# Layer two of a graph network: three picked tiles in every superblock, 64-slot bins in column halves, rows returned as PSUM sums

## The chip, the cores and the metric

The kernel is one program on one core of a Trainium2 chip. Its engines are TensorE (PE in the rows, its weight loads PEld), VectorE (DVE), ScalarE (ACT), GpSimd (POOL) and SyncE (SP), which run side by side and wait for each other by semaphores. The metric is the time of one execution on the device in microseconds, the median of several runs.

## What is computed

Two layers on a graph of 6250 nodes and 200000 edges, the edges sorted by target. Layer one is a normalised sum over neighbours. Layer two, which the change is about, forms a message for every edge and sums the messages by target:

```python
x = x + _L0_gnn_ref(h, edge_index, L0_gnn_W, L0_gnn_b)        # layer one
h = jnp.maximum(_layernorm(x, axis=-1), 0.0)
...
source_x = jnp.take(node_x, sources, axis=0)                  # layer two
target_x = jnp.take(node_x, targets, axis=0)
message_in = jnp.concatenate((source_x, target_x, edge_x), axis=1)
message_x = relu(message_in @ msg_W1 + msg_b1) @ msg_W2 + msg_b2
agg = jax.ops.segment_sum(message_x, targets, num_segments=num_nodes)
update_in = jnp.concatenate((agg, node_x), axis=1)
return relu(update_in @ upd_W1 + upd_b1) @ upd_W2 + upd_b2
```

The source part of the first product is made once for every node: a table a of 6250 rows of 64 numbers. A message before its ReLU is then the source's row of a, plus the target's row of a second table b, plus the edge's own features times a 64x64 weight.

## The kernel before

**Tiling.** Edges are taken in tiles of 128 (one edge a partition) and in superblocks of T = 8 tiles, NSB = 196 superblocks in all. Four superblocks (U = 4, slots k = 0 to 3) make one trip of the loop that every engine runs over layer two, 49 trips. Each engine has its instructions in an order written out by hand (`step`), with parts of later superblocks ahead of those of the current one.

**Two ways to a source row.** Most tiles are gathered: POOL issues one indirect DMA for each tile of 128 rows (L684), from indices that SP loads. Of every 32 tiles POOL gathers 22 (slots 0 and 1 whole, six tiles of slot 3). The other ten (all of slot 2, two of slot 3; `KPE`, `PT`, `GTS`) are picked on PE, in two groups g of five tiles a trip. A group's 640 edges are put into 7 bins of source nodes (896 nodes each) with 128 slots a bin, by ranks that are worked out ahead of layer one. One group then takes these stages:
- DVE marks each edge's slot and bin (L1093 to L1096), PE packs the sources into slots (`pack_slots`, L1727: five products of 7 columns), DVE copies them (L1101);
- PE spreads them over the partitions (`spread_slot_src`, L1738: seven transposing products of 128 columns), ACT copies (L1405);
- DVE builds the one-hot matrices `pick` (L1109: seven of 896 columns), PE multiplies them with the table a held in bf16 in three parts (`pick_rows`, L1760: 49 products, 128 slots by 192 columns), ACT copies (L1414);
- DVE builds `from_slot` (L1118: seven of 640 columns), PE brings the rows from slots back to edges (`return_rows`, L1774: 5 tiles by 7 bins = 35 products of 192 columns), DVE adds the three parts into `rows` (`build_rows`, L1127).

**A superblock's own work.** SP loads its edge features, indices and window of b. DVE writes its target one-hots (L905). PE transposes both together (`transpose_edges`, L1692: 8 fp32 products of 128 columns) two steps ahead, ACT copies them (L1392). `edge_and_target_terms` (L1702) makes 16 fp32 products of 64 columns into bank 2 or 3; each has 64 weight columns and fills one half of the partitions, left and right half in turn, and the trace shows two instructions for each fp32 product with a 64-wide weight, 32 in all. DVE adds the source rows (`add_rows`, L1137), ACT applies ReLU (L1397), PE sums the messages by target (`sum_messages`, L1712: 8 such products, 16 instructions), DVE adds the window's sums into `acc` (L1144).

**Order.** In PE's step k: `spread_slot_src` if k is even, then `transpose_edges`, then `pack_slots` and half of `pick_rows` if k is odd, `edge_and_target_terms`, then `return_rows` (k even) or the rest of `pick_rows` (k odd), then `sum_messages`. DVE is strictly in order: `add_rows` stands ahead of picks, copies and one-hots of later superblocks.

**Ahead of layer one.** POOL works out bins and running counts (L626 to L648), PE the ranks (L1518, L1519), ACT copies them, POOL forms codes and the crowding flag (L651 to L678). If a bin held more edges than slots, layer two would be repeated in rounds (`ROUNDS`).

## Time and profile before

| | |
|---|---|
| median of 3 runs | 2338.83 us (2332.95 to 2340.99) |
| the profiled execution | 2333.39 us, of it 2331.6 us in the span of its profile |
| set-up up to the first gather of layer one | 0 to 199 us |
| layer one | 199 to 800 us |
| between the layers | 800 to 863 us |
| layer two, 196 superblocks | 863 to 2293 us |
| update and output | 2293 to 2332 us |
| busy shares of the span | PE 88%, PEld 77%, DVE 72%, POOL 70%, ACT 49% |

The busy time of a stretch of PE reaches from its first product's start to its last one's modelled end, and a single product lasts far longer than the distance to the next one, so distances are worked out from starts. For POOL a gather counts as busy while it is prepared; what passes between two gathers is put down as idle time with the releaser "issue". A letter "ld" behind PE means weight loads. A wait names the engine and line that came last.

### The profile page before, as it was taken

Reading aid. Unit: us, or ns where it says so; the run is one execution under the profiler, and the core shown is the slowest. Engines: PE = TensorE matmul, PEld = TensorE weight load, DVE = VectorE, ACT = ScalarE, POOL = GpSimd, SP = SyncE. Lnnn points to the kernel's source line nnn. Section 1 sums busy time; section 2 is a strip of 40 time slices with the busy share of each in tenths; the row PEclk is TensorE's granted clock in tenths of the full one; section 3 lists DMA queues with packets and bytes.
Section 4 is the critical chain, followed back from the end, with each engine's and each line's share of the span. In section 5 each row is a group of like instructions: output and inputs, shape, how many; then the busy total and the mean of one; then the engine's idle time right before and its main releaser. Section 6 shows DMA issues by size and latency. Waiting matters only on the chain.

```text
span 2331.6 us, 79009 instructions
## 1 busy us (share of the span) xinstructions
PE 2043.8 (88%) x26825; PEld 1784.7 (77%) x26826; DVE 1687.9 (72%) x4590; ACT 1147.5 (49%) x2411; POOL 1628.0 (70%) x1577
## 2 busy tenths in 40 slices
PE   2156999999999949999999999999999999999997
PEld 1144788887888748888888888888888888888884
DVE  8866788887888686776667666666666677666662
ACT  0003888888888644444444444444444444444432
POOL 4465777777777127777777777777777777777771
PEclk6566999999999969999999999999999999999998
DMA  3001111111111133333333333333333333333332
GB/s 75 1 1 42 27 27 28 28 28 28 25 27 28 9 76 68 78 80 74 75 75 75 75 75 75 75 75 75 75 75 75 77 78 76 74 74 74 76 73 39
DMA packets 346919, 133.38 MB, mean 57 GB/s; under 512 B 305501, under 2 KB 322755, under 8 KB 346787
## 3 DMA queue, kind: packets, MB, share of 16 engines
q1 hardware_dynamic: 298980, 82.66, 15.9%
q0 software_dynamic: 47808, 49.05, 11.7%
q8 instruction: 72, 1.18, 0.2%
q14 instruction: 59, 0.48, 0.1%
HBM read 124.04 MB, written 7.52 MB: 56 GB/s over the span
## 4 chain that ended last, share of the span: by engine, by line
PE 54%; DVE 15%; issue 13%; POOL 10%; DMA 4%; DVEq 3%; ACT 1%; SPq 1%; POOLq 0%; PEld 0%; PEldq 0%; ACTq 0%
PE psum L1570 12%; PE psum L1760 12%; POOL rows L684 9%; PE psum L1602 9%; DVE H L1109 4%; PE psum L1774 4%; PE psum L1702 4%; PE psum L1712 3%; PE psum L1591 2%; DMA rows<-a_rows,idx 2%; PE psum L1692 2%; DVEq L1148 2%; DMA idx<-src_by_tile 2%; DVE rows L1127 1%; PE psum L1581 1%
## 5 line engine op out<-in xcount | busy, mean ns | idle before, releaser
L684 POOL DMA_INDIRECT rows<-a_rows,idx x1078 | 1088.9, 1010 | 374.8 <-issue 360.3
L1339 ACT ACTIVATE hT<-psum 128x392 bf16<-128x392 f32 x1152 | 510.6, 502 | 101.3 <-PE psum L1602 93.2
L684 POOL DMA_INDIRECT rows<-g_rows,idx x416 | 425.9, 1024 | 152.5 <-issue 125.6
L1760 PE MATMUL psum<-edge_index,H 128*128 128x192 bf16 x4802 | 429.8, 246 | 61.0 <-DVE Y L1101 59.4
L1570 PE MATMUL psum<-work,hT 128*128 128x192 bf16 x3528 | 455.9, 247 | 0.3 <-ACT hT L1339 0.3
L1760 PEld LDWEIGHTS psum<-edge_index,H 128*128 128x128 bf16 x4802 | 389.8, 98 | 70.7 <-issue 65.7
L1392 ACT ACTIVATE eoT<-psum 128x512 f32<-128x512 f32 x392 | 213.8, 603 | 351.6 <-PE psum L1692 348.0
L1570 PEld LDWEIGHTS psum<-work,hT 128*128 128x128 bf16 x3528 | 324.3, 99 | 70.9 <-issue 1.4
L1602 PE MATMUL psum<-Z,one_lo 128*128 128x392 f16 x1152 | 365.4, 339 | 14.6 <-DVE Z L946 14.5
L1414 ACT ACTIVATE Y<-psum 128x384 bf16<-128x384 f32 (+1 forms) x392 | 176.5, 450 | 308.5 <-PE psum L1760 297.3
L1774 PE MATMUL psum<-Y,Z 128*128 128x192 bf16 x3430 | 307.7, 246 | 0.9 <-ACT Y L1405 0.9
L946 DVE TENSOR_SCALAR Z<-digit,edge_index 128x392 f16<-128x392 f16 x1152 | 296.9, 328 | 0.0
L1774 PEld LDWEIGHTS psum<-Y,Z 128*128 128x128 bf16 x3430 | 285.4, 98 | 7.7 <-ACT Y L1405 1.1
L1109 DVE TENSOR_SCALAR H<-Y,node_cmp 128x896 bf16<-128x896 f16 x686 | 261.2, 451 | 6.9 <-ACT Y L1405 6.8
L1137 DVE TENSOR_TENSOR msg<-psum,rows 128x512 f32<-128x512 f32 x196 | 134.4, 686 | 149.7 <-DMA rows<-a_rows,idx 118.3
L1702 PE MATMUL psum<-wb,eoT 128*64 128x64 f32 x6272 | 226.6, 225 | 0.0
L1118 DVE TENSOR_SCALAR Z<-Z,slot_cmp 128x640 bf16<-128x640 f16 x686 | 225.3, 397 | 0.0
L1702 PEld LDWEIGHTS psum<-wb,eoT 128*64 128x64 f32 x6272 | 199.5, 138 | 31.6 <-issue 31.6
L905 DVE TENSOR_TENSOR work<-iota_bw,rel 128x512 f32<-128x512 f32 x196 | 135.7, 693 | 118.5 <-issue 118.5
L1692 PE MATMUL psum<-ident,work 128*128 128x128 f32 x1568 | 211.7, 278 | 0.0
L1602 PEld LDWEIGHTS psum<-Z,one_lo 128*128 128x128 bf16 x1152 | 160.3, 145 | 36.2 <-DVE Z L946 25.6
L1397 ACT ACTIVATE msg<-msg 128x512 f32<-128x512 f32 x196 | 123.2, 629 | 110.3 <-DVE msg L1137 94.0
(272 smaller groups left out, 1961.5 us busy)
## 6 DMA issues: line engine op xcount, KB each, us to landing
work<-in_edge_attr_dram SPq DMA_DIRECT2D x392, 128.0 KB
rows<-a_rows,idx POOLq DMA_INDIRECT x1078
Z<-slot_code SPq DMA_DIRECT2D x98, 160.0 KB
rows<-g_rows,idx POOLq DMA_INDIRECT x416
idx<-src_by_tile SPq DMA_DIRECT2D x200, 4.0 KB
wb<-b_rows SPq DMA_DIRECT2D x196, 16.0 KB, 2.3
g_rows<-Y SPq DMA_DIRECT2D x1, 1600.0 KB, 8.9
a_rows<-Y SPq DMA_DIRECT2D x6, 256.0 KB, 2.6
```

The lines of the kernel that those rows point to most:

```text
L684: pool.indirect_dma_start(out=rows[:, k, t, :], out_offset=None, in_=table, in_offset=bass.IndirectOffsetOnAxis(ap=idx[:, k, t:t + 1], axis=0)
L946: V.tensor_scalar(keys[:, g * T + t, :], key_digit[:, :], key_of[:, bass.ds(tile + t, 1)], None, ALU.is_equal).then_inc(key_ready, 1)
L1109: ins = V.tensor_scalar(pick[:, b, :], slot_src[:, :], node_cmp[:, b:b + 1], None, ALU.is_equal)
L1118: ins = V.tensor_scalar(from_slot[:, b, 0:cols], code_row[:, g, 0:cols], slot_cmp[:, b:b + 1], None, ALU.is_equal)
L1339: nc.scalar.activation(counts[:, j % 2, :, t * SLOTS:(t + 1) * SLOTS], psum[:, t % 4, 0:KEYS].rearrange("p (h m) -> p h m", m=SLOTS), ACT.Copy
L1392: nc.scalar.activation(eoT[:, k % 2, h * 4:h * 4 + 4, :], psum[:, h, :].rearrange("p (t e) -> p t e", e=P), ACT.Copy).then_inc(eoT_ready, 1)
L1570: ins = TT.matmul(psum[:, 4 + (j + 1) % 2, 0:NPART * D], counts[:, (j + 1) % 2, h, :], gtab[:, h, :, :].rearrange("p k d -> p (k d)"), sta ...
L1602: TT.matmul(psum[:, t % 4, 0:KEYS], one_lo[:, t // T, :, t % T], keys[:, t, :], start=True, stop=True).then_inc(counted, 1)
L1692: ins = TT.transpose(psum[:, h, (t % 4) * P:(t % 4 + 1) * P], eo[:, k, t, :], ident[:, :])
L1702: ins = TT.matmul(psum[half:half + D, 2 + k % 2, t * D:(t + 1) * D], eoT[:, k % 2, t, half:half + D], wb[:, k, :], start=True, stop=True)
L1760: ins = TT.matmul(psum[:, PICK_BANK[u], (b % 2) * NPART * D:(b % 2 + 1) * NPART * D], pick[:, h, b * P:(b + 1) * P], atab[:, b * BLK + h, ...
L1774: ins = TT.matmul(psum[:, bank, (t - t0) * NPART * D:(t - t0 + 1) * NPART * D], from_slot[:, b, t * P:(t + 1) * P], picked_rows[:, b, :], ...
```

## The change

Every superblock is now alike. POOL gathers its first five tiles, PE picks the last three (`PG` = 5, `PT` = 3), so a trip of four superblocks has 20 gathered and 12 picked tiles. A superblock's 384 picked edges go into 10 bins of 640 nodes with 64 slots each, two bins to a chunk of 128 slots (`CHUNKS` = 5).

- `pick_rows`: a bin's product has 64 weight columns and goes to one half of the partitions; left and right bin alternate: 5 chunks x 5 blocks x 2 halves = 50 products of 192 columns a superblock.
- `picked_tiles` takes the place of `return_rows` and `build_rows`: for each picked tile PE first writes the edge and target terms into the message bank (two fp32 products of 64 columns in halves), then adds 5 chunks x 3 parts = 15 products of 64 columns with the whole array's weights onto the same 64 columns. No DVE reduction is left; DVE adds gathered rows for five tiles only, and ACT's ReLU reads three tiles straight from PSUM.
- The stages run for every superblock (`for_stages` with offsets of up to four steps), with two buffers each. `pack_slots` now waits for the copy of the first picked bank of superblock j+2 (it shares bank 7), which stands behind `relu` of j+1 on ACT.
- In a step of PE the transposes come first, then the spread.
- Bins are found by integer shifts and one-hots on DVE, right behind the sources' transposition; the ranks are reduced by DVE out of PSUM, and POOL starts its chain after that. A product of one-hot and source for every picked edge and chunk (`chunk_src`) is made by POOL between the layers.
- SP loads indices of five tiles, one code DMA of three tiles a superblock.

The core of the diff:

```diff
-    KPE = 2
-    POOL_SLOTS = [k for k in range(U) if k != KPE]
-    GTS = (5, 5)
-    PT = sum(GTS)
-    GOFF = (0, GTS[0])
-    GT = max(GTS)
-    GE = GT * P
-    PE0 = KPE * T
-    PIECES = [([(7, 4, 1)] if n == 5 else []) + [(5, 0, 2), (6, 2, 2)] for n in GTS]
-    NPIECE = sum(len(p) for p in PIECES)
-    GATHERS = [T - max(0, min(T, PE0 + PT - k * T)) if k >= KPE else T for k in range(U)]
-    BINS = 7
-    BLK = HS // BINS
+    PT = 3
+    PG = T - PT
+    CAP = D
...
+    BINS = 10
+    BLK = 5
     BIN_NODES = BLK * P
-    SLOTS_G = BINS * P
-    NPT = NIT * PT
-    ROUNDS = GE // P
-    CENTRE = 2 * SLOTS_G
-    LAST = 4
-    LAST_BASE = 4096 - LAST * SLOTS_G + CENTRE
+    CHUNKS = BINS * CAP // P
...
+    NPT = NSB * PT
+    GE = PT * P
+    ROUNDS = GE // CAP
...
+    SPREAD_BANK = (5, 6)
+    PICK_BANK = (7, 6, 5)
+    PACK_BANK = 7
+    NPICK = len(PICK_BANK)
+    LEAD = 4
...
+        def for_stages(eng, step):
+
+            for k in range(-LEAD, 0):
+                step(0, k)
+            with eng.Fori(0, NIT - 1) as i:
+                for k in range(U):
+                    step(i, k)
+            for k in range(U):
+                step(NIT - 1, k)
...
+                for t in range(PG if ring == 1 else T):
...
+            for c in range(CHUNKS):
+                ins = G.tensor_scalar(chunk_src[:, :, c], pe_chunk, float(c), None, ALU.is_equal)
+            link(ins)
+            G.tensor_tensor(chunk_src, chunk_src, wide(pe_src.rearrange("p (n c) -> p n c", c=1), 2, CHUNKS),
+                            ALU.mult).then_inc(s_chunksrc, 1)
...
+            link(V.tensor_scalar(div_i.rearrange("p (s t) -> p s t", t=PT), pe_tiles, 7, None, ALU.logical_shift_right))
+            link(V.tensor_scalar(div_i, div_i, float(1024 // BLK + 1), None, ALU.mult))
+            link(V.tensor_scalar(bin_i, div_i, 10, None, ALU.logical_shift_right))
+            V.tensor_scalar(chunk_i, bin_i, 1, None, ALU.logical_shift_right)
+            link(V.tensor_copy(bin16, bin_i))
+            for b in range(BINS):
+                ins = V.tensor_scalar(bin_oh[:, :, b, :], bin16.rearrange("p (q t) -> p q t", t=RT), float(b), None, ALU.is_equal)
+            ins.then_inc(s_binoh, 1)
...
+            for q in range(NR // 2):
+                dve.wait_ge(s_rank, q + 1)
+                V.tensor_reduce(rank32[:, 2 * q * RT:2 * (q + 1) * RT].rearrange("p (a t) -> p a t", t=RT),
+                                psum[:, 2 * (q % 2):2 * (q % 2) + 2, 0:BINS * RT].rearrange("p a (b t) -> p a t b", t=RT),
+                                AX, ALU.max).then_inc(s_rankc, 1)
+            dve.wait_ge(s_rankc, NR // 2)
+            link(V.tensor_reduce(far_max[:, :], rank32, AX, ALU.max))
...
+                        for work_, ahead_ in ((onehots_of, 3), (ranks_of, 4), (slots_to_edges, 2), (add_rows, 1), (picks, 3),
+                                              (copy_packed, 4), (add_sums, 0)):
+                            to = at(i, k, ahead_)
+                            if to is not None:
+                                work_(*to)
...
+                    act.wait_ge(added, n + 1 + U)
+                    nc.scalar.activation(msg[:, k % 2, 0:PG, :], msg[:, k % 2, 0:PG, :], ACT.Relu).then_inc(relu_done, 1)
+                    nc.scalar.activation(msg[:, k % 2, PG:T, :],
+                                         psum[:, 2 + k % 2, PG * D:T * D].rearrange("p (t d) -> p t d", d=D), ACT.Relu
+                                         ).then_inc(relu_done, 1)
...
+                    for work_, ahead_ in ((hold_chunks, 4), (copy_transposed, 2), (copy_slot_src, 3), (relu, 1), (copy_picked, 2)):
...
+                def edge_and_target_terms(k, t, alone):
+                    for half in (0, D):
+                        ins = TT.matmul(psum[half:half + D, 2 + k % 2, t * D:(t + 1) * D], eoT[:, k % 2, t, half:half + D],
+                                        wb[:, k, :], start=True, stop=alone)
+                    return ins
+
+                def gathered_tiles(i, k):
                     n = r * NSB + i * U + k
                     pe.wait_ge(b_in[k], 16 * (r * NIT + i + 1))
-                    for t in range(T):
+                    for t in range(PG):
                         if t % 4 == 0:
                             pe.wait_ge(eoT_ready, 2 * n + t // 4 + 1)
-                        for half in (0, D):
-                            ins = TT.matmul(psum[half:half + D, 2 + k % 2, t * D:(t + 1) * D], eoT[:, k % 2, t, half:half + D],
-                                            wb[:, k, :], start=True, stop=True)
-                    ins.then_inc(pre_done, 1)
+                        edge_and_target_terms(k, t, True)
+
+                def picked_tiles(i, k):
+                    n = r * NSB + i * U + k
+                    pe.wait_ge(from_slot_ready, n + 3)
+                    pe.wait_ge(picked_copied, NPICK * (n + 1))
+                    for t in range(PT):
+                        edge_and_target_terms(k, PG + t, False)
+                        to = psum[:, 2 + k % 2, (PG + t) * D:(PG + t + 1) * D]
+                        for c in range(CHUNKS):
+                            for h in range(NPART):
+                                ins = TT.matmul(to, from_slot[:, k % 2, c, t * P:(t + 1) * P],
+                                                picked_rows[:, k % 2, c, h * D:(h + 1) * D],
+                                                start=False, stop=(c == CHUNKS - 1 and h == NPART - 1))
+                    ins.then_inc(returned, 1)
...
                     pe.wait_ge(ranked, n + 1)
-                    if not opening(i, g):
+                    pe.wait_ge(chunk_held, n + 1)
+                    if not opening(i, k):
+                        pe.wait_ge(picked_copied, NPICK * (n - 2) + 1)
...
+                        for c in range(2 * u, min(2 * u + 2, CHUNKS)):
+                            for h in range(BLK):
+                                for half in range(2):
+                                    ins = TT.matmul(psum[half * CAP:(half + 1) * CAP, PICK_BANK[u],
+                                                         (c % 2) * NPART * D:(c % 2 + 1) * NPART * D],
+                                                    pick[:, k % 2, h, c * P + half * CAP:c * P + (half + 1) * CAP],
+                                                    atab[:, (2 * c + half) * BLK + h, :, :].rearrange("p k d -> p (k d)"),
+                                                    start=(h == 0), stop=(h == BLK - 1))
+                        ins.then_inc(picked, 1)
...
+                    for work_, ahead_ in ((transpose_edges, 2), (spread_slot_src, 3), (gathered_tiles, 1), (picked_tiles, 1),
+                                          (pick_rows, 2), (pack_slots, 4), (sum_messages, 0)):
+                        to = at(i, k, ahead_)
+                        if to is not None:
+                            work_(*to)
```

PE's order in an even step of the loop, from the transposes (`work`) over the target and edge terms (`wb,eoT`) and the returned rows (`Y,Z`) to the sum of messages, before:

```order
L1692 MATMUL psum<-ident,work 128x128 x8
L1700 REGISTER_ALU
L1702 MATMUL psum<-wb,eoT 64x64 x8
L1700 REGISTER_ALU
L1702 MATMUL psum<-wb,eoT 64x64 x8
L1767 REGISTER_ALU
L1768 REGISTER_ALU
L1770 REGISTER_ALU
L1774 MATMUL psum<-Y,Z 128x192 x35
L1712 MATMUL psum<-work,msg 64x64 x8
```

and in every step now, from the first target and edge terms up to the picked rows (`edge_index,H`), which the products of 64 columns come ahead of:

```order
L1645 MATMUL psum<-wb,eoT 64x64 x8
L1654 REGISTER_ALU
L1645 MATMUL psum<-wb,eoT 64x64 x4
L1666 MATMUL psum<-Y,Z 128x64 x15
L1645 MATMUL psum<-wb,eoT 64x64 x2
L1666 MATMUL psum<-Y,Z 128x64 x15
L1645 MATMUL psum<-wb,eoT 64x64 x2
L1666 MATMUL psum<-Y,Z 128x64 x15
L1716 MATMUL psum<-edge_index,H 64x192 x20
L1712 REGISTER_ALU
L1716 MATMUL psum<-edge_index,H 64x192 x30
```

The one group of 35 full products of 192 columns became three groups of 15 products of 64, each behind two products in halves; the products in halves that pick rows (64x192) stand in every step.

DVE's order in step k = 0 before, from the target one-hots over `add_rows` to the three reductions of returned rows:

```order
L905 TENSOR_TENSOR work<-iota_bw,rel 128x8x64
L1135 ISA
L1136 REGISTER_ALU
L1137 TENSOR_TENSOR msg<-psum,rows 128x512
L1106 ISA
L1107 ISA
L1109 TENSOR_SCALAR H<-Y,node_cmp 128x896 x7
L1125 ISA
L1127 TENSOR_REDUCE rows<-psum 128x64
L1125 REGISTER_ALU
L1127 TENSOR_REDUCE rows<-psum 128x128
```

and in every step now, from the target one-hots to the five one-hots for picking:

```order
L916 TENSOR_TENSOR work<-iota_bw,rel 128x8x64
L1086 ISA
L1086 TENSOR_TENSOR Y<-digit,tmp_e 128x384
L1106 ISA
L1108 REGISTER_ALU
L1110 TENSOR_SCALAR Z<-Z,slot_cmp 128x384 x5
L1119 REGISTER_ALU
L1120 REGISTER_ALU
L1121 TENSOR_TENSOR msg<-psum,rows 128x320
L1097 REGISTER_ALU
L1098 ISA
L1100 TENSOR_SCALAR H<-Y,node_cmp 128x640 x5
```

The reductions are gone, `add_rows` covers 320 columns, and slot marks and `from_slot` (`slot_cmp`) stand ahead of it.

## Rows read from the trace of the kernel before

**Rows 1.** Windows: busy time by engine, clock, DMA share and GB/s, layer two.

```profile
core 0: us, PE busy (x) PEld busy (x) DVE busy (x) ACT busy (x) POOL busy (x), PEclk, DMA share, GB/s
900.00:2290.00 1390.00, 1292.02 (x19970) 1176.55 (x19967) 954.77 (x2573) 578.75 (x1149) 1063.66 (x1054) 1.00 0.36 75
```

**Rows 2.** Groups by form, 900 to 2290 us, POOL: count, busy, mean ns, idle before.

```profile
L684 POOL DMA_INDIRECT rows<-a_rows,idx x1054 | 1063.7, 1009 | 322.2 <-issue 311.4 <-DMA idx<-src_by_tile 10.8
```

**Rows 3.** Waits, 900 to 2290 us: us in total, times, longest.

```profile
DVE msg L1137 <- DMA rows<-a_rows,idx: 118.3, 35, 5.3
...
PE psum L1760 <- DVE Y L1101: 59.4, 42, 1.9
```

**Rows 4.** Timeline of PE, two steps: start, us, line, form, count, idle before.

```profile
1502.64 0.56 PE L1738 MATMUL psum<-ident,Y 128*128 128x128 f16 x7
1503.05 1.04 PE L1692 MATMUL psum<-ident,work 128*128 128x128 f32 x8
1504.02 1.15 PE L1702 MATMUL psum<-wb,eoT 128*64 128x64 f32 x32
1505.10 3.14 PE L1774 MATMUL psum<-Y,Z 128*128 128x192 bf16 x35
1508.17 0.69 PE L1712 MATMUL psum<-work,msg 128*64 128x64 f32 x16
1508.79 1.09 PE L1692 MATMUL psum<-ident,work 128*128 128x128 f32 x8
1510.11 0.28 PE L1727 MATMUL psum<-Y 128*128 128x7 f16 x5 [0.22 <-DVE Y L1096]
1510.33 2.47 PE L1760 MATMUL psum<-edge_index,H 128*128 128x192 bf16 x28
1512.73 1.15 PE L1702 MATMUL psum<-wb,eoT 128*64 128x64 f32 x32
1513.81 1.91 PE L1760 MATMUL psum<-edge_index,H 128*128 128x192 bf16 x21
1515.65 0.69 PE L1712 MATMUL psum<-work,msg 128*64 128x64 f32 x16
1516.36 0.34 PE L1738 MATMUL psum<-ident,Y 128*128 128x128 f16 x3
```

**Rows 5.** Groups by form, 900 to 2290 us, PE: mean ns of one product.

```profile
L1760 PE MATMUL psum<-edge_index,H 128*128 128x192 bf16 x4659 | 415.7, 246 | 59.4 <-DVE Y L1101 59.4
...
L1727 PE MATMUL psum<-Y 128*128 128x7 f16 x470 | 26.2, 169 | 28.1 <-DVE Y L1096 28.0
```

**Rows 6.** Timeline of PE in layer one: 16 instructions in one half only.

```profile
791.79 1.15 PE L1591 MATMUL psum<-eoT,rows 128*64 128x64 f32 x16
```

**Rows 7.** Groups by form, 900 to 2290 us, DVE and ACT.

```profile
L1109 DVE TENSOR_SCALAR H<-Y,node_cmp 128x896 bf16<-128x896 f16 x665 | 253.2, 451 | 0.0
L1118 DVE TENSOR_SCALAR Z<-Z,slot_cmp 128x640 bf16<-128x640 f16 x665 | 218.4, 397 | 0.0
L1137 DVE TENSOR_TENSOR msg<-psum,rows 128x512 f32<-128x512 f32 x194 | 133.0, 686 | 149.7 <-DMA rows<-a_rows,idx 118.3 <-PE psum L1702 30.8 <-issue 0.6
...
L1397 ACT ACTIVATE msg<-msg 128x512 f32<-128x512 f32 x193 | 121.3, 629 | 104.4 <-DVE msg L1137 88.1 <-issue 10.2
```

**Rows 8.** Groups by form, 55.9 to 84 us (set-up), DVE.

```profile
L799 DVE TENSOR_SCALAR slot_node<-slot_node,slot 128x104 f32<-128x104 f32 x1 | 5.9, 5928 | 0.0
L762 DVE TENSOR_TENSOR bad<-bad,general 128x1 f32<-128x1 f32 x3 | 5.4, 1788 | 0.1
L801 DVE CAST slot_abs_i<-slot_node 128x104 int32<-128x104 f32 x1 | 3.3, 3296 | 0.0
L800 DVE COPY slot_abs<-slot_node 128x104 f32<-128x104 f32 x1 | 3.3, 3291 | 0.0
...
L809 DVE TENSOR_SCALAR fast<-general 128x1 f32<-128x1 f32 x1 | 0.2, 153 | 0.0
```

**Rows 9.** Timeline: first and last sum of messages.

```profile
892.80 0.69 PE L1712 MATMUL psum<-work,msg 128*64 128x64 f32 x16
...
2291.29 1.12 PE L1712 MATMUL psum<-work,msg 128*64 128x64 f32 x16 [5.41 <-ACT msg L1397]
```

More of the change, by code:

```diff
@@ L235, in gnn_two_layers @@
[L235 to L239 removed]
+        o = NPT * BINS // 2
+        bin_oh = acc[:, 0:o].bitcast(bf16).rearrange("p (q b t) -> p q b t", b=BINS, t=RT)
+        scratch = [acc[:, q * NPT:(q + 1) * NPT] for q in range(5)]
@@ new lines, in copy_picked @@
+                def copy_picked(i, k):
+                    n = r * NSB + i * U + k
+                    if not opening(i, k):
+                        act.wait_ge(returned, n - 1)
+                    for u in range(NPICK):
+                        m = min(2, CHUNKS - 2 * u)
+                        act.wait_ge(picked, NPICK * n + u + 1)
+                        nc.scalar.activation(picked_rows[:, k % 2, 2 * u:2 * u + m, :],
+                                             psum[:, PICK_BANK[u], 0:m * NPART * D].rearrange("p (c d) -> p c d", c=m), ACT.Copy
+                                             ).then_inc(picked_copied, 1)
@@ L1688, in transpose_edges @@
                     for h in range(2):
-                        if not first:
+                        if not (isinstance(i, int) and i * U + k == 0):
                             pe.wait_ge(eoT_ready, 2 * n - 1 + h)
@@ L1714, in sum_messages, with pack_slots @@
                     ins.then_inc(summed[1], 1)
-                def pieces_of(i, g):
-                    return NPIECE * (r * NIT + i) + (len(PIECES[0]) if g else 0)
-                def pack_slots(i, g):
-                    n = 2 * (r * NIT + i) + g
+                def pack_slots(i, k):
+                    n = r * NSB + i * U + k
                     pe.wait_ge(ranked, n + 1)
-                    if not opening(i, g):
-                        pe.wait_ge(slot_src_copied, 2 * n)
-                    if not (isinstance(i, int) and i == 0):
-                        pe.wait_ge(rows_built, pieces_of(i, 0) if g else pieces_of(i - 1, 1))
-                    for t in range(GTS[g]):
-                        ins = TT.matmul(psum[:, 6, 0:BINS], rank_oh[:, g, t, :], bin_src[:, g, t, :],
-                                        start=(t == 0), stop=(t == GTS[g] - 1))
-                    ins.then_inc(packed, 1)
```

636 lines of the change are left out of this document (239 added, 397 removed).

## The prediction

> **What bounds the kernel now.** I read the windows first. Over 1390 us of layer two PE is busy 1292 us, 93%, at the full clock, 1.00 or 2.4 GHz; POOL is busy 1064 us, which looks like slack [rows 1]. It isn't. Between two gathers lies an idle piece with the releaser "issue", and busy time plus idle time of the gathers is 1063.7 + 322.2 = 1385.9 us [rows 2]: POOL never rests. A gather costs 1385.9 / 1054 = 1.315 us, 22 a trip of four superblocks 28.9 us, 7.23 us a superblock. The sums of messages agree: from first to last (2291.29 - 892.80) / 195 = 7.17 us [rows 9]. The waits show how it reaches the others: DVE's `add_rows` waits 118 us for gathers, and PE's picks wait 59 us for a small copy (L1101) that stands behind `add_rows` on DVE [rows 3].
>
> PE's own pace is read from two steps of the timeline [rows 4]. The even one, from 1502.64 to 1508.79, has no wait: 6.15 us. The odd one lasts to 1516.36, 7.57 us, of which about 0.5 is waiting (its transposes would let `pack_slots` start at 1509.67, not 1510.11, and 0.09 ahead of the next step). So PE needs 6.6 us a superblock and is given 7.2. Two bounds lie 0.6 us apart.
>
> **POOL, part by part.** 20 gathers a trip instead of 22, at 1.315 us: 26.3 us, **6.58 us a superblock**. Whatever PE needs beyond that is now the pace, and POOL's saving of 0.65 us a superblock (127 us in all) can be had only down to PE's own time.
>
> **PE, prices.** The distance between two products of a group is (busy - one product) / (count - 1). Picks: (2.47 - 0.246) / 27 = 0.082 us for 192 columns; returns (3.14 - 0.246) / 34 = 0.085; `pack_slots` (0.28 - 0.169) / 4 = 0.028, a load of 128x128 fp16 weights with 7 columns behind it [rows 4, 5]. Spread: 0.41 us to the next group for 7, 0.058. Transposes: 8 in 0.97 with the turn below, 0.11. For products in halves two groups give slope and constant: 32 in 1.08 us (1504.02 to 1505.10), 16 in 0.62 (1508.17 to 1508.79): **0.029 each and 0.16 a visit**. Full-width groups ahead of them leave 0.09 too: 28 picks take 2.40 where 28 x 0.082 is 2.31, 35 returns 3.07 against 2.98 [rows 4]. So a change from whole array to halves and back costs 0.25 us, and there were two in a step.
>
> **PE's new step**, in the order shown above, start to start:
> - transposes 8 x 0.11 = 0.88; spread 5 x 0.058 + 0.09 = 0.38
> - terms of five gathered and the first picked tile, 24 x 0.029 + 0.16 = 0.86
> - three groups of returns, 3 x (15 x r + 0.09). A bf16 product of 64 columns with whole weights is not in the trace. Below, 0.028 (`pack_slots`: its weight load alone); above, 0.058 (spread, 128 columns). I take r = 0.0305, next to the halves' 0.029 with the same 64 columns: 1.64
> - terms of two more tiles, 2 x (4 x 0.029 + 0.16) = 0.55
> - picks: 25 pairs x p + 0.16. The pair too is absent. The evidence that halves overlap is in fp32: 16 instructions in one half only are busy 1.15 us [rows 6], 16 that alternate 0.69 [rows 4]; a pair costs what one costs. Below p = 0.082, above two in a row, 0.164. I take 0.085: 2.29
> - pack 3 x 0.028 + 0.07 = 0.15; sum of messages 0.62
>
> Together **7.37 us**, of it 1.25 for five changes of width instead of two. Returned columns fell (3 x 15 x 64 = 2880 a superblock against 17.5 x 192 = 3360), the changes of width eat more than that, and picking costs as many column times as before (25 against 24.5 products' worth). The same prices give 6.6 for the old step, as measured.
>
> The Trainium skill speaks against the picks at this price: "TensorEngine Tiling (Array Packing)", section "Restrictions and Gotchas", says that column tiling excludes the fast weight load, and "TensorE: Matmul & The Clock Gate", section "LDWEIGHTS (loading the stationary operand)", gives columns / 1.2 ns, an estimate of 53 ns for 64. Two such loads in a row are 0.107 us a pair, and the step would be 0.55 us longer. No run here shows a bf16 load in halves.
>
> Against slow loads the trace has the fp32 groups: two loads of 64 columns and two products fit into 2 x 0.029 = 0.058 us, under 0.085 [rows 4].
>
> **DVE and ACT beside it.** DVE's busy time for one 640-column one-hot is 218.4 / 665 = 0.33 us, for 896 columns 0.38 [rows 7], so 384 columns some 0.27. A step: 5 x 0.33 + 5 x 0.27 + `add_rows` on 320 columns 0.5 (0.686 for 512) + two one-hot operations 1.2 + copies and sums 0.4 + reading the window's base 0.6 = 5.7 us, under 7.37. The removed reductions were off the path. The new wait is at `pack_slots`: queued behind it on PE are `sum_messages` and the next step. Returns end 4.4 us into the step, `add_rows` 5.0, two ReLUs (0.629 for 512 columns in one [rows 7], here 0.47 and 0.33) 5.8, the copy of the first picked bank 6.3; PE reaches pack at 6.6. It fits by 0.3 us. Putting transposes first gives the copy of the packed slots 0.88 us of cover; I price it at nothing. SP issues one more code DMA for two superblocks, and its DMAs have a whole step's time; DMA share was 0.36 [rows 1].
>
> **Layer two.** From first to last sum: 193 steps x 7.37 + 4.4 for the two short last ones = 1426.8 us against 1398.5 [rows 9], +28. The first sum comes some 6 us earlier, with four partial steps of filling instead of the old hand-written opening (from -10 to +3). PE stays busy to the end: the last sum's 16 instructions took 1.12 us where they took 0.69 at the full clock [rows 9], so about -2. Sum +20.
>
> **Ahead of it.** In set-up DVE runs tiny operations beside POOL's bin work at 5.9, 5.4, 3.3 and 3.3 us where one takes 0.15 [rows 8]: 17.9 - 1.0 = 17 us that go, since POOL now waits there for the ranks; smaller ones beside them may bring 3 to 5 more. Added on DVE: five integer operations at about 0.45 and ten one-hots at 0.35, 6 us, and the wait for PE's ranks with seven reductions out of PSUM ahead of the layer norm, about 9. POOL's later chain can hold up the layer norm as it did before, less by a guess of 3. Net -8, between -18 and +3. Between the layers POOL's 12 us of `chunk_src` runs beside DVE's serial chain: 0 to +6, I take +3.
>
> **Sum.** +20 - 8 + 3 = +15 us. The profiled execution (2333.4 us) becomes 2348; the median lay 5.4 us above that execution, so 2338.8 + 15 = **2354 us**. The point from which it is neutral is a step of 7.29 us.
>
> **Rivals.**
> - *The change is faster.* One mechanism: the unmeasured products run at their lower bounds. r = 0.028 takes 0.11 us a step, p = 0.082 0.08, and a return group, whose last product is short, leaves the array some 0.05 sooner: 7.13 us, 193 x 0.24 = 46 us less, 2308. For it: every bound is a row. Against: fp32 pairs show no product in halves cheaper than 0.029, and any overlap lost costs at once. It decides below 7.25.
> - *The pack's wait bites.* If the chain of DVE and ACT is 0.6 us longer than drawn (semaphores, POOL holding up DVE), PE stands 0.3 us a step: +58, 2412.
> - *Weight loads bound the picks.* If a pair costs two full products of the smallest kind that has its own load, 2 x 0.058 = 0.116, the step grows by 25 x 0.031 = 0.78: +150, 2504. The page's figure above would give 2460.
> - *Halves don't overlap* for bf16: p = 0.164, +1.98 us a step, +381, 2735. Against it rows 6.
> - *A bin overflows*: one superblock with over 64 picked edges in a bin turns on six rounds. The reference's own inputs reach 64 exactly, so it fits.
>
> **How the numbers follow.** My forecast (step 7.26 to 7.48, 2332 to 2376) has 0.55. Faster at the lower bounds 0.23, pack's wait 0.10, weight loads 0.06, halves in series 0.05, overflow 0.01. The range goes from 2310, which takes in nearly all of the first rival, to 2405, half of the second: it leaves out about 0.18. A measurement of this kernel can tell 0.3%, 7 us. Of the forecast's own range, 2332 to 2346 is 0.17 and a little is below: faster 0.24, within 0.17, slower 0.59.
>
> **What would show it.** Step by step in the profile after: 980 gathers at 1.3 us with waits for indices between them, POOL's share down; PE at 99% or more in layer two, without idle time ahead of picks; sums of messages 7.3 to 7.5 us apart; 15 returns in 0.55 us start to start; 50 picks in 2.3; DVE's small operations back at 0.2 us in set-up. A group of 50 picks at 2.7 or more, or idle time of PE ahead of `pack_slots` released by ACT, would make the prediction wrong upwards; a step under 7.25 us downwards.

## The result, and the profile after

The changed kernel takes **2353.4 us** (median of 5 runs, 2350.2 to 2355.8), the kernel before 2339.5 us (5 runs): ratio 1.0062, 95% interval 1.0044 to 1.0080. It is slower by 14 us, as forecast (2354). The profiled execution took 2353.4 us, its span is 2351.6 us: by the spans alone the change cost 20.0 us, by the medians 13.9, because the profiled execution of before lay 6 us under its median and this one lies on it. The working in the prediction was made against the spans and said +15.

Busy time, clock and DMA share of layer two in the changed kernel, in windows (us, then busy us of PE, PEld, DVE, ACT, POOL; clock, DMA share, GB/s):

```profile
core 0: us, PE busy (x) PEld busy (x) DVE busy (x) ACT busy (x) POOL busy (x), PEclk, DMA share, GB/s
900.00:2290.00 1390.00, 1385.79 (x29795) 1249.31 (x29791) 903.22 (x2813) 691.95 (x1878) 924.46 (x944) 1.00 0.36 73
```

Against [rows 1] PE went from 1292 to 1386 busy us of 1390, and POOL from 1064 to 924. The waits of the same stretch (engine and line, released by; us in total, times, longest) have no row of PE at all, where before had 59 us ahead of the picks [rows 3]. POOL, which never rested [rows 2], now waits for its indices:

```profile
engine line waited for: us in total, times, longest us
...
DVE msg L1121 <- PE psum L1666: 270.6, 187, 1.7
POOL rows L672 <- issue: 235.1, 766, 1.5
POOL rows L672 <- DMA idx<-src_by_tile: 230.5, 178, 1.6
```

So the bound moved from POOL to PE. One step of PE in the timeline (start, us, line, form, count), the counterpart of [rows 4]:

```profile
1502.43 1.09 PE L1640 MATMUL psum<-ident,work 128*128 128x128 f32 x8
1503.36 0.44 PE L1701 MATMUL psum<-ident,Y 128*128 128x128 f16 x5
1503.73 0.92 PE L1645 MATMUL psum<-wb,eoT 128*64 128x64 f32 x24
1504.58 0.65 PE L1666 MATMUL psum<-Y,Z 128*128 128x64 bf16 x15
1505.16 0.34 PE L1645 MATMUL psum<-wb,eoT 128*64 128x64 f32 x4
1505.43 0.65 PE L1666 MATMUL psum<-Y,Z 128*128 128x64 bf16 x15
1506.00 0.34 PE L1645 MATMUL psum<-wb,eoT 128*64 128x64 f32 x4
1506.27 0.65 PE L1666 MATMUL psum<-Y,Z 128*128 128x64 bf16 x15
1506.85 2.25 PE L1716 MATMUL psum<-edge_index,H 128*64 128x192 bf16 x50
1509.03 0.23 PE L1688 MATMUL psum<-chunk_cur,Y 128*128 128x5 f16 x3
1509.19 0.69 PE L1677 MATMUL psum<-work,msg 128*64 128x64 f32 x16
1509.81 1.09 PE L1640 MATMUL psum<-ident,work 128*128 128x128 f32 x8
```

Start to start, transposes to transposes, it is 7.38 us; the prediction's sum was 7.37:

| group | predicted us | measured us |
|---|---|---|
| transposes | 0.88 | 0.93 |
| spread | 0.38 | 0.37 |
| terms of gathered and first picked tile | 0.86 | 0.85 |
| three groups of 15 returns | 1.64 | 0.58 + 0.57 + 0.58 = 1.73 |
| terms of two more tiles | 0.55 | 0.27 + 0.27 = 0.54 |
| 25 pairs of picks | 2.29 | 2.18 |
| pack | 0.15 | 0.16 |
| sum of messages | 0.62 | 0.62 |

The return is dearer than taken (0.032 us instead of 0.0305), the pair of picks is not: 0.0825 us from one pair to the next (the starts in the trace lie 0.079 and 0.0035 us apart in turn), the lower bound, and what one 192-column product cost before. The two misses and the transposes cancel to 0.03.

Where the 20 us of span lie, by landmarks in the two traces. The chain of work that ended last has the same group, 49 products ahead of the end of layer one, at 790.88 instead of 800.56 us, and the first terms of the source and target rows between the layers at 832.12 instead of 838.55 us (start, us, what; first after, then before):

```profile
790.88 4.22 PE psum L1518 x49
832.12 3.65 PE psum L1599 x16
```

```profile
800.56 4.22 PE psum L1570 x49
838.55 3.65 PE psum L1651 x16
```

And the sums of messages, first and last, in the timeline of PE after (before's are in [rows 9]):

```profile
878.79 0.69 PE L1677 MATMUL psum<-work,msg 128*64 128x64 f32 x16
...
2314.06 0.69 PE L1677 MATMUL psum<-work,msg 128*64 128x64 f32 x16 [0.76 <-ACT msg L1362]
```

| stretch | before us | after us | change | predicted |
|---|---|---|---|---|
| set-up and layer one, to that group | 800.6 | 790.9 | -9.7 | -8 |
| from there to the rows between the layers | 38.0 | 41.2 | +3.3 | +3 |
| from there to the first sum | 54.3 | 46.7 | -7.6 | -6 |
| first to last sum | 1398.5 | 1435.3 | +36.8 | +28 |
| last sum to the end | 40.3 | 37.5 | -2.8 | -2 |

In set-up the trace shows what the prediction named: POOL runs nothing between 50 and 110 us, since it waits for the ranks, and the small operations on DVE are small again (groups by form, 55.9 to 84 us, DVE; [rows 8] had 1788, 5928, 3291 and 3296 ns):

```profile
L756 DVE TENSOR_TENSOR bad<-bad,general 128x1 f32<-128x1 f32 x3 | 0.5, 159 | 0.1
L802 DVE TENSOR_SCALAR slot_node<-slot_node,slot 128x104 f32<-128x104 f32 x1 | 0.3, 276 | 0.0
L803 DVE COPY slot_abs<-slot_node 128x104 f32<-128x104 f32 x1 | 0.2, 215 | 0.0
L804 DVE CAST slot_abs_i<-slot_node 128x104 int32<-128x104 f32 x1 | 0.2, 215 | 0.0
```

The work that set-up gained was not measured by itself, only the net of -9.7.

### The profile page after: what moved, and what is told of

Its sections match the earlier page's. It is cut to its first block, busy times and chain, and to the rows that moved or that the text cites. A ratio compares the mean times of both kernels' runs of the same rounds, so it can differ in the third digit from the quotient of the medians.

```text
span 2351.6 us, 102122 instructions
## 1 busy us (share of the span) xinstructions
PE 2171.0 (92%) x37635; PEld 1887.0 (80%) x37635; DVE 1642.8 (70%) x4904; ACT 1274.7 (54%) x3188; POOL 1480.3 (63%) x1462
## 4 chain that ended last, share of the span: by engine, by line
PE 90%; DVE 6%; issue 2%; ACT 1%; POOL 0%; DMA 0%; DVEq 0%; PEldq 0%; ACTq 0%; SPq 0%; POOLq 0%
PE psum L1716 18%; PE psum L1666 14%; PE psum L1518 12%; PE psum L1645 11%; PE psum L1550 9%; PE psum L1640 9%; PE psum L1677 5%; PE psum L1539 2%; PE psum L1701 2%; PE psum L1688 1%; PE psum L1529 1%; PE psum L1484 1%; DVE work L833 1%; PE psum L1745 0%; PE psum L1746 0%
## 5 line engine op out<-in xcount | busy, mean ns | idle before, releaser
L672 POOL DMA_INDIRECT rows<-a_rows,idx x980 | 961.4, 981 | 512.9 <-issue 281.4
L1716 PE MATMUL psum<-edge_index,H 128*64 128x192 bf16 x9800 | 442.4, 247 | 0.0
L1716 PEld LDWEIGHTS psum<-edge_index,H 128*64 128x64 bf16 x9800 | 400.2, 110 | 10.5 <-issue 0.2
L1550 PE MATMUL psum<-Z,lo_hi 128*128 128x392 f16 x1152 | 365.0, 339 | 19.2 <-DVE Z L956 19.2
L1666 PE MATMUL psum<-Y,Z 128*128 128x64 bf16 x8820 | 380.0, 194 | 0.0
L1100 DVE TENSOR_SCALAR H<-Y,node_cmp 128x640 bf16<-128x640 f16 x980 | 328.9, 401 | 0.4 <-ACT Y L1355 0.4
L1121 DVE TENSOR_TENSOR msg<-psum,rows 128x320 f32<-128x320 f32 x196 | 96.4, 492 | 287.8 <-PE psum L1666 287.8
L1110 DVE TENSOR_SCALAR Z<-Z,slot_cmp 128x384 bf16<-128x384 f16 x980 | 257.9, 328 | 0.4 <-DMA Z<-slot_code 0.4
L1550 PEld LDWEIGHTS psum<-Z,lo_hi 128*128 128x128 bf16 x1152 | 160.5, 145 | 40.9 <-DVE Z L956 30.1
L1640 PEld LDWEIGHTS psum<-ident,work 128*128 128x128 f32 x1568 | 168.4, 141 | 20.4 <-issue 10.5
```

What stands on the lines that cost most here:

```text
L672: pool.indirect_dma_start(out=rows[:, k, t, :], out_offset=None, in_=table, in_offset=bass.IndirectOffsetOnAxis(ap=idx[:, k, t:t + 1], axis=0)
L1100: ins = V.tensor_scalar(pick[:, k % 2, h, :], slot_src[:, k % 2, :], node_cmp[:, h:h + 1], None, ALU.is_equal)
L1110: ins = V.tensor_scalar(from_slot[:, k % 2, c, :], code_row[:, k % 2, :], slot_cmp[:, c:c + 1], None, ALU.is_equal)
L1550: TT.matmul(psum[:, t % 4, 0:KEYS], one_lo[:, t // T, :, t % T], keys[:, t, :], start=True, stop=True).then_inc(counted, 1)
L1640: ins = TT.transpose(psum[:, h, (t % 4) * P:(t % 4 + 1) * P], eo[:, k, t, :], ident[:, :])
L1666: ins = TT.matmul(to, from_slot[:, k % 2, c, t * P:(t + 1) * P], picked_rows[:, k % 2, c, h * D:(h + 1) * D], start=False, stop=(c == CHUN ...
```

## The experiments

The question is whether the sum was right for its reasons: that POOL bounded the kernel before, that halves overlap, that a turn between whole array and halves costs 0.25 us, that two product widths have the prices taken, and that pack's chain has room. There are twelve runs of nine kernels. Seven of them fell on two chips on which the kernel before takes 1.6 times its time (3690 and 3762 us, granted clock 0.77 to 0.83 over the run instead of 0.95). Three of these kernels were run again, and two more for the first time, on two chips where the kernel before took 2339.2 and 2333.5 us. First the five runs there:

| kernel | median us | ratio to before, 95% interval | step of PE, us |
|---|---|---|---|
| before, 18 gathers a trip | 2272.5 | 0.9739 (0.9721 to 0.9757) | 6.15 and 7.6 |
| picks in one half | 2753.5 | 1.1803 (1.1782 to 1.1823) | 9.44 |
| picks whole | 2309.1 | 0.9895 (0.9876 to 0.9914) | 7.15 |
| terms first | 2252.0 | 0.9628 (0.9610 to 0.9647) | 6.87 |
| one visit | 2166.8 | 0.9263 (0.9246 to 0.9279) | 6.37 |

The step is the median distance of the sums of messages in each trace, within a trip of four superblocks; for the changed kernel it is 7.38.

**Did POOL bound the kernel before?** In the kernel before one gathered tile a superblock is left out:

```diff
-for t in range(T - GATHERS[k] if ring == 1 else 0, T):
+for t in range(T - GATHERS[k] + 1 if ring == 1 else 0, T):
```

> The kernel of before_18g again, on a chip on which the kernel before takes its 2339 us: one gathered tile left out in every superblock of layer two (stale rows in its place), 18 gathers a trip instead of 22. Theory: POOL set the pace of before; with 5.9 us of gathers a superblock PE's own 6.6 us show, 111 us less, about 2228 us. Rival: PE or DVE set it all along, 2339 us.

It fell by 61 us, not by 111. POOL did bound: with fewer gathers the time falls, and POOL now waits for indices (168 us of 1300). But PE doesn't get down to 6.6 us. In the timeline of this kernel the odd steps are as long as they were in [rows 4], and ahead of `pack_slots` PE waits for the product on DVE that marks the bins (L1096). On DVE this product stands behind the reductions of returned rows, and no wait for a gather is left in this trace:

```profile
1511.36 0.69 PE L1712 MATMUL psum<-work,msg 128*64 128x64 f32 x16
...
1517.51 0.69 PE L1712 MATMUL psum<-work,msg 128*64 128x64 f32 x16
1518.13 1.09 PE L1692 MATMUL psum<-ident,work 128*128 128x128 f32 x8
1519.60 0.28 PE L1727 MATMUL psum<-Y 128*128 128x7 f16 x5 [0.38 <-DVE Y L1096]
...
1525.15 0.69 PE L1712 MATMUL psum<-work,msg 128*64 128x64 f32 x16
```

The two steps are 6.15 and 7.64 us, a mean of 6.9. Of the 0.6 us a superblock that the prediction saw between PE and POOL, half was POOL's and half a wait of the old order itself, which the changed order doesn't have.

**Do the halves overlap?** The pairs of picks all write into the first column half:

```diff
-for h in range(BLK):
-    for half in range(2):
-        ins = TT.matmul(psum[half * CAP:(half + 1) * CAP, PICK_BANK[u],
+for half in range(2):
+    for h in range(BLK):
+        ins = TT.matmul(psum[0:CAP, PICK_BANK[u],
```

> The changed kernel, but all 50 picking products of a superblock write into the first column half (so the second half of the picked slots is stale). Same number of instructions, weights and columns. Theory: a pair in two halves runs at the same time, one product in 0.082 us; in one half they queue, 50 x 0.082 instead of 25: 25 x 0.082 = 2.05 us a step more, 196 x 2.05 = 402 us, about 2755 us. Rival: a product in halves costs 0.041 us by itself (half the array, half the work, or bound by its weight load), so nothing overlaps and the time stays 2353 us.

2753.5 us, beside 2755 expected, and the group of 50 shows it (timeline of PE):

```profile
1505.68 4.31 PE L1716 MATMUL psum<-edge_index,H 128*64 128x192 bf16 x50
1509.92 0.23 PE L1688 MATMUL psum<-chunk_cur,Y 128*128 128x5 f16 x3
```

4.24 us for 50 in one half, 2.18 for 50 in alternate halves. A product in a half costs what one in the whole array costs (0.083 us from one to the next, against 0.082), and two in different halves cost that together. Both kernels load the same weights. The Trainium skill, "TensorE: Matmul & The Clock Gate", section "LDWEIGHTS (loading the stationary operand)", gives columns / 1.2 ns, an estimate of 0.107 us for a pair if its two loads of 64 columns follow each other. The trace has 0.0825 with both loads in it, so the rival of weight loads falls, by measurement.

**Does the turn cost what was taken?** In one kernel each pair of picks is a single product with whole weights:

```diff
-for half in range(2):
-    ins = TT.matmul(psum[half * CAP:(half + 1) * CAP, PICK_BANK[u],
+for half in range(1):
+    ins = TT.matmul(psum[:, PICK_BANK[u],
...
-                    pick[:, k % 2, h, c * P + half * CAP:c * P + (half + 1) * CAP],
+                    pick[:, k % 2, h, c * P:(c + 1) * P],
```

> The changed kernel, but each pair of picking products is replaced by one with whole weights of 128 columns and the table rows of the first half's bin (so the second half of the slots picks from wrong rows). 25 products instead of 50, and the picks stand between returns and pack in the whole array: one turn to halves and back less. Theory: the pair costs what one costs, so the picks themselves gain nothing (0.082 each), and the turn's 0.25 us goes: a step of 7.13 us, 196 x 0.25 = 49 us less, 2304 us. Rival: the turn costs nothing by itself and the pairs pay for their instructions: any gain comes inside the group, a product under 0.082 us.

The step fell by 0.23 us and the time to 2309.1 us on a chip whose kernel before is 6 us under the other's. In its timeline the group holds no gain beyond the turn, 2.06 us for 25, which is 0.0825 each; the returns ahead of it are 0.09 shorter (from 1500.07 to 1500.55, where they took 0.58), the picks 0.12:

```profile
1500.07 0.65 PE L1666 MATMUL psum<-Y,Z 128*128 128x64 bf16 x15
1500.55 2.22 PE L1716 MATMUL psum<-edge_index,H 128*128 128x192 bf16 x25
1502.61 0.22 PE L1688 MATMUL psum<-chunk_cur,Y 128*128 128x5 f16 x3
```

In another nothing of the computation changes, only the order. The terms of all eight tiles come first, then the 45 returns; the message bank is one accumulation group, opened by the first term of each half and closed by the last return:

```diff
-for t in range(PG):
+for t in range(T):
     ...
-    edge_and_target_terms(k, t, True)
+    edge_and_target_terms(k, t, t < PG)
...
-wb[:, k, :], start=True, stop=alone)
+wb[:, k, :], start=(t == 0), stop=False)
...
-    edge_and_target_terms(k, PG + t, False)
...
-start=False, stop=(c == CHUNKS - 1 and h == NPART - 1))
+start=False, stop=(t == PT - 1 and c == CHUNKS - 1 and h == NPART - 1))
```

> The kernel of terms_first again, for the same reason. Two turns from whole array to halves and back go at 0.25 us each: a step of 6.88 instead of 7.38 us, 2255 us. Rival: the gaps belong to the dependence of a return on the term just written, and stay: within 20 us of 2353.

2252.0 us beside 2255 expected, a step of 6.87 beside 6.88. This kernel is 87 us faster than the one before. With a step order in which the three groups in halves are neighbours it goes on:

```diff
-for work_, ahead_ in ((transpose_edges, 2), (spread_slot_src, 3), (gathered_tiles, 1), (picked_tiles, 1),
-                      (pick_rows, 2), (pack_slots, 4), (sum_messages, 0)):
+for work_, ahead_ in ((transpose_edges, 2), (spread_slot_src, 3), (picked_tiles, 1), (pick_rows, 2),
+                      (sum_messages, 0), (gathered_tiles, 2), (pack_slots, 4)):
```

> The kernel of one_visit again, on a chip on which the kernel before takes its 2339 us (the first chip gave it 3690 us, with idle pieces of TensorE that no instruction explains). Same expectation as there: PE's own pace 6.4 us a step with one turn to halves instead of five, POOL 6.58 us for five gathers, so a step of 6.6 us and about 2200 us. Rival: DVE's chain takes over at 7 us or more, 2280 us or above. If the time is again above 3500 us, this chip is throttled too and nothing follows for the step.

**2166.8 us, 172 us under the kernel before** and 187 under the changed one. PE's step is 6.37 us, the 6.4 of the expectation; one step of its timeline:

```profile
1505.12 1.07 PE L1640 MATMUL psum<-ident,work 128*128 128x128 f32 x8
1506.02 0.44 PE L1700 MATMUL psum<-ident,Y 128*128 128x128 f16 x5
1506.30 1.58 PE L1665 MATMUL psum<-Y,Z 128*128 128x64 bf16 x45
1507.82 2.25 PE L1715 MATMUL psum<-edge_index,H 128*64 128x192 bf16 x50
1509.90 0.63 PE L1676 MATMUL psum<-work,msg 128*64 128x64 f32 x16
1510.37 0.81 PE L1645 MATMUL psum<-wb,eoT 128*64 128x64 f32 x22
```

This order also tells a turn from its rival, that a product waits for the one before it whose result it adds to. Spread takes 0.37 us to the next group where terms in halves follow (in the changed kernel) and 0.28 where returns follow; the sum of messages takes 0.62 where transposes follow and 0.47 where terms follow. No group here adds to the result of the one ahead of it, and the two differences, 0.09 and 0.15, are the two parts of the 0.25.

The expectation was too high by 33 us. Some 22 of them lie in POOL, which it held at 1.315 us a gather, 6.58 a superblock. A gather's busy time here is 990 ns instead of 1009, with the same 0.3 us between two (groups by form, 900 to 2100 us, POOL):

```profile
L672 POOL DMA_INDIRECT rows<-a_rows,idx x928 | 918.5, 990 | 283.1 <-issue 268.5 <-DMA idx<-src_by_tile 14.6
```

(918.5 + 283.1) / 928 = 1.295 us, 6.47 a superblock, which is also what the sums of messages give over whole trips: three steps of 6.37 and one of 6.74. POOL all but never rests, and PE is busy 1190 of 1200 us. Still, the pace is PE's: without its waits for indices POOL needs (918.5 + 268.5) / 928 = 1.279 us a gather, 6.40 a superblock. The long fourth step is PE's too. Its groups take what they take in the other steps, except that from pack to transposes, where one trip of the loop ends and the next begins, there are 0.44 us instead of 0.09. What the transposes wait for there had been given over 4 us earlier:

```profile
1543.63 0.23 PE L1687 MATMUL psum<-chunk_cur,Y 128*128 128x5 f16 x3
1544.07 1.09 PE L1640 MATMUL psum<-ident,work 128*128 128x128 f32 x8 [0.21 <-issue]
```

So this turn of the loop costs PE 0.37 us, and in the changed kernel it costs 0.15. What makes the difference is open.

**The runs on the two slow chips.** The same three kernels on the first of them, and one more with 4 gathers in the one-visit order:

> The kernel before, with one gathered tile left out in every superblock of layer two (18 gathers a trip of four superblocks instead of 22, so its sums for those tiles use stale rows). My theory: POOL set the pace of before (1.315 us x 22 = 28.9 us a trip, 7.23 us a superblock), and PE alone needs 6.6. With 18 gathers POOL needs 5.9, so the pace falls to PE's 6.6: 195 x (7.17 - 6.6) = 111 us less, about 2228 us, and the step pairs of 6.15 and 7.6 stay while the long steps of 9 us at a trip's start go. Rival: PE or DVE set the pace and POOL was only busy beside them: no change, 2339 us.

> The changed kernel, with the terms of all eight tiles written ahead of the 45 returns, in one accumulation group for the message bank, instead of alternating tile by tile. The computation is the same. My theory: a turn from whole array to halves and back costs 0.25 us, and three of five such turns in a step sit around the picked tiles; two of them go: the step falls from 7.38 to 6.88 us, 196 x 0.5 = 98 us less, 2255 us. Rival: the gaps belong to the dependence of a product on the one before it in the same bank (a return adds onto a term just written), so the order does not matter or it costs elsewhere: within 20 us of 2353.

> As the kernel with all eight terms ahead of the returns, and PE's step written in another order: transposes (+2), spread (+3), returns (+1), then the three groups in halves side by side, picks (+2), sum of messages (0), terms (+2), and last pack (+4). One turn to halves in a step instead of five: 4 x 0.25 = 1.0 us off 7.38, PE's own pace 6.4 us. Then POOL is the later one: 5 gathers x 1.315 = 6.58 us a superblock. My theory: a step of 6.6 us, 2353 - 195 x 0.8 = about 2200 us, POOL without waits for indices, PE with waits for DVE's rows. Rival: DVE's chain (copy of packed slots now last on PE, sum's addition behind it, then the next one-hots) takes over, a step of 7 us or more: 2280 us or above.

> The one-visit order with 4 gathers a superblock instead of 5 (a gathered tile uses stale rows). POOL then needs 5.3 us. My theory: PE's own pace shows, 6.4 us a step, 40 us less than with 5 gathers, about 2160 us. Rival (DVE sets it): same time as with 5 gathers.

Against 3689.5 us for the kernel before they took 3541.7, 3896.9, 3906.0 and 3483.4 us. The two orders whose steps differ by 0.50 us above differ here by nothing that stands out of the noise (3897 and 3906), and the sums of messages lie 13.3 us apart on average in both. Against their own times on the other chips the three kernels take 1.56, 1.73 and 1.80 times as long. The timeline of PE in the one-visit kernel:

```profile
2011.91 0.20 PE L1687 MATMUL psum<-chunk_cur,Y 128*128 128x5 f16 x2 [0.24 <-issue]
2012.66 0.38 PE L1640 MATMUL psum<-ident,work 128*128 128x128 f32 x2 [0.55 <-issue]
2014.10 0.38 PE L1640 MATMUL psum<-ident,work 128*128 128x128 f32 x2 [1.06 <-issue]
2015.54 1.10 PE L1640 MATMUL psum<-ident,work 128*128 128x128 f32 x3 [1.07 <-issue]
```

Between products of one group PE stands for over 1 us, released by nothing that the profile shows. From 1300 to 3400 us such pauses come to 417 us in this kernel and 481 in the one with terms first, and the granted clock changes to and fro between 1.2 and 2.4 GHz, 0.77 on average. So a step there is made up of pauses and half clock, and its length doesn't tell what the groups cost. What causes the pauses was not found. With 4 gathers the time fell by 11%, to 3483 us; why fewer gathers weigh that much there was not found, and whether they would bring anything on the other chips was not run.

The last three kernels fell on the second slow chip and were not run again; the changed kernel itself was not run there. The five tiles' ReLU in five pieces:

```diff
-nc.scalar.activation(msg[:, k % 2, 0:PG, :], msg[:, k % 2, 0:PG, :], ACT.Relu).then_inc(relu_done, 1)
+for t in range(PG):
+    ins = nc.scalar.activation(msg[:, k % 2, t, :], msg[:, k % 2, t, :], ACT.Relu)
+ins.then_inc(relu_done, 1)
```

> The changed kernel with the ReLU over the five gathered tiles' messages (320 columns, 0.47 us) written as five of 64 columns. The computation is the same. Theory (the rival of the waiting pack): ahead of PE's pack stands a chain of returns, add_rows, two ReLUs and the copy of the first picked bank; in the trace of the changed kernel that copy ends 0.4 us before pack begins. Five small activations at 0.2 to 0.25 us (one of 15 columns takes 0.21) make the chain 0.5 to 0.75 us longer, so pack waits 0.1 to 0.35 us a step with ACT as releaser: 20 to 70 us more, about 2390 us. Rival: the chain has more room than that, or other work of ACT gives way, and the time stays 2353 us.

It took 3978.4 us against 3761.9, which says nothing of pack. What can be read is the chain's length, since DVE's and ACT's durations are the same on that chip (the copy of the transposes takes 597 ns, in the changed kernel 596). First the timeline of ACT in the changed kernel, then in this one:

```profile
1507.55 0.47 ACT L1361 ACTIVATE msg<-msg 128x320 f32<-128x320 f32 x1 [2.62 <-DVE msg L1121]
1507.92 0.31 ACT L1362 ACTIVATE msg<-psum 128x192 f32<-128x192 f32 x1
1508.13 1.34 ACT L1373 ACTIVATE Y<-psum 128x384 bf16<-128x384 f32 x3
```

```profile
2005.46 0.84 ACT L1362 ACTIVATE msg<-msg 128x64 f32<-128x64 f32 x5 [4.49 <-DVE msg L1121]
2006.20 0.31 ACT L1364 ACTIVATE msg<-psum 128x192 f32<-128x192 f32 x1
2006.41 0.48 ACT L1375 ACTIVATE Y<-psum 128x384 bf16<-128x384 f32 x1
```

From the first ReLU to the copy of the first bank 0.58 us, here 0.95: 0.37 longer, not 0.5 to 0.75. In the changed kernel that copy ends at 1508.13 + 0.48 = 1508.61 and pack begins at 1509.03, 0.42 us of room. By these two numbers the edit would have fitted into it on a chip at full clock, which was not run; the point at which pack begins to wait was not reached by any run.

Returns with half the columns:

```diff
-ins = TT.matmul(to, from_slot[:, k % 2, c, t * P:(t + 1) * P],
-                picked_rows[:, k % 2, c, h * D:(h + 1) * D],
+ins = TT.matmul(to[:, 0:D // 2], from_slot[:, k % 2, c, t * P:(t + 1) * P],
+                picked_rows[:, k % 2, c, h * D:h * D + D // 2],
```

> The changed kernel with 32 columns instead of 64 in each of the 45 returns of a superblock (the upper half of each message gets no picked row). A return of 64 columns takes 0.032 us to the next, pack's product of 5 columns with whole weights 0.028 or less. Theory: at 64 columns the return is bound by its columns and just above its weight load, so half the columns bring it down only to the load's 0.026 us or so: 45 x 0.006 = 0.27 us a step, 53 us less, 2300 us. Rival 1: columns alone count, 0.019 us: 0.6 us a step, 2238 us. Rival 2: the load alone bounds it already at 64 columns: 2353 us.

3864.8 us against 3761.9, a time that says as little as the others there. The prices can be read from the trace. Most returns ran at half clock, and their distance has one value in most places: 0.027 us with 32 columns, where the kernels with 64 columns on the same chip have 0.053. Both are the columns at 1.2 GHz (26.7 and 53.3 ns). The last steps of layer two ran at full clock (1.00 from 3813 to 3828 us):

```profile
3814.09 0.54 PE L1666 MATMUL psum<-Y,Z 128*128 128x32 bf16 x15
3814.57 0.34 PE L1645 MATMUL psum<-wb,eoT 128*64 128x64 f32 x4
3814.83 0.54 PE L1666 MATMUL psum<-Y,Z 128*128 128x32 bf16 x15
```

Fifteen returns take 0.47 to 0.48 us instead of 0.58, and most lie 0.025 us apart instead of 0.032. That is 3 x 0.107 = 0.32 us a step, near the 0.27 expected: half the columns bring less than half, and the rival by which columns alone count (0.019) falls at this clock. So the load of whole bf16 weights takes at most 0.025 us. Whether the load or something else sets 0.025, and what bounds 64 columns at 0.032 and not at the 26.7 ns of the columns, is open.

Spread ahead of transposes, which takes back the last part of the change:

```diff
-for work_, ahead_ in ((transpose_edges, 2), (spread_slot_src, 3), (gathered_tiles, 1), (picked_tiles, 1),
+for work_, ahead_ in ((spread_slot_src, 3), (transpose_edges, 2), (gathered_tiles, 1), (picked_tiles, 1),
```

> The changed kernel with spread (+3) ahead of transposes (+2) in PE's step: this takes back the part of the change that put the transposes first. The computation is the same. Theory: the copy of the packed slots on DVE ends 0.28 us after pack's last product and PE sums messages for 0.62 us in between, so spread finds it ready; two whole-array groups only change places: within 10 us of 2353. Rival: that copy stands behind other work of DVE often enough, PE then waits ahead of spread, 0.3 us a step or more: 2410 us.

3978.8 us, level with the ReLU in pieces on that chip (3978.4), and its trace has no wait of PE ahead of spread. That fits the expectation of no difference but doesn't show it: on a chip where reordering has no price, equality is weak evidence.

## Why the prediction was right, point by point

- **The bound moves from POOL to PE.** Shown by the waits after (PE has none) and by the run with fewer gathers. The step in it that failed is "PE needs 6.6 us a superblock and is given 7.2": without POOL's bound the kernel before runs at 6.9, since a wait of its own order, which the prediction read in [rows 4] as waiting that would go, takes half of the difference. It had no effect on the forecast, which compared the new step with the measured 7.17.
- **The new step, 7.37 us.** Measured 7.38. Of its two unknown products one came out above what was taken (returns, 0.032) and one at its lower bound (picks, 0.0825); each alone would have moved the time by about 20 us (0.09 and 0.11 us a step, 196 steps).
- **A turn costs 0.25 us.** Shown twice, once by making the picks whole (0.23) and once by order alone: 0.51 for two turns and 1.01 for four. This was the term that made the change a loss. Five turns instead of two are 0.75 us a step or 147 us; without them the same work is faster than before.
- **Halves overlap.** Shown by taking the overlap away: 2.05 us a step expected, 9.44 - 7.38 = 2.06 measured.
- **Pack's wait.** It did not occur. The chain had 0.42 us of room where the prediction drew 0.3. **Weight loads** did not bound the picks either (0.0825 us a pair).
- **Layer two, +28 from first to last sum.** Measured +36.8. The step was sized right; left out was the turn from one trip to the next, 0.15 us every fourth step. 48 of them (0.154 us each in the trace) are 7.4 of the 8.5 us between the 1426.8 of the prediction and the 1435.3 measured. The kernel before has 0.10 us at the same place (steps of 6.25 beside 6.15), where the prediction could have read it.
- **Set-up, filling and the stretch between the layers** were -9.7, -7.6 and +3.3 us where -8, -6 and +3 were said. They were near as sums; no run takes their terms apart.
- **The last digits are luck.** That the trips' 7.4 us don't show in the final number comes of this: the prediction carried the 5.4 us between the profiled execution and the median over to the changed kernel, whose profiled execution lies on its median.

## What to carry to other kernels

- When an engine is the bound, price the order of its groups, not only their products. Here one TensorE turn from whole-array to half-array products and back cost 0.25 us whatever stood in the groups, and putting all half-array groups of a step side by side gained 187 us with the same products.
- Before moving work off the engine that bounds the kernel, look how near the next one is, and whether it has waits of its own order that stay when the first bound goes: they were half of the apparent distance here.
- Two half-array products in alternate halves cost what one costs, at both widths measured here (64 columns in fp32, 192 in bf16). Two in the same half cost twice that. Halving the array gains only if the pair does useful work.

## What the runs showed of the hardware that was not expected

- A turn between whole and half array costs TensorE 0.25 us there and back, with fp32 or bf16 in the halves (0.23 to 0.26 us in three kernels).
- The turn of the loop costs TensorE 0.15 us a trip in the changed kernel and 0.37 in the one-visit kernel, with nothing to wait for.
- An indirect gather has no quite fixed price: without waits for indices 1.305 us from one to the next in the kernel before, 1.276 in the same kernel with 18 gathers a trip, 1.279 in the one-visit kernel. What moves it by 2% was not found; the DMA share was 0.36, 0.35 and 0.42.
- Chips differ. On two of the four that the experiments ran on, kernels took 1.56 to 1.80 times their time, with TensorE standing over 1 us inside a group and a granted clock of 0.77 to 0.83 over the run. There two orders of TensorE's groups that differ by 4% elsewhere took the same time, and the kernel that is 7% faster elsewhere was 6% slower than before.
